# One attention kernel, two orders of the scores within a slot: two pairs and two, or three pairs and one

## The chip, the cores and the metric

The kernel runs on one core of one Trainium2 chip. The metric is the device time of one launch in microseconds (us), the median of several runs. TensorE (PE in the profile, PEld for its weight loads) multiplies matrices into PSUM. VectorE (DVE) and ScalarE (ACT) read PSUM and work element by element. GpSimd (POOL) adds a little, and SyncE (SP) issues most of the DMAs. The engines run side by side and meet only at semaphores.

## The reference

Per image of 512 tokens and 256 features (16 images, 16 heads of 16 features), with `x` in float32:

```python
q = heads(x @ Wq)
k_s, v_s = heads(x @ Wkv_short)        # keys and values of the short attention
decay_bias = -abs(pos[None, :] - pos[:, None]) * (1.0 - decay_factor)
out_short = softmax(q k_s^T / 4 + decay_bias) v_s
k_l, v_l = heads(x @ Wkv_long)
out_long = softmax(q k_l^T / 4) v_l
out = alpha * out_short + (1 - alpha) * out_long     # alpha = sigmoid(mix_weight)
x = layernorm(x + out @ Wo)
# then a gated recurrence over the 16 images, an output layer and a second layernorm
```

Both orders compute the same: first attention with the largest score of each row taken off before the exponential, then the recurrence.

## The kernel before

The launch has two phases. The attention phase (`attention_phase`) takes four fifths of the time. The recurrence phase (`recurrence_phase`) follows it and is not touched.

The attention phase handles one image per `body(b)`, with b from -1 to 16, all written out. A body has 32 **slots**. The work of an image is eight units of four heads, alternately of the long and of the short attention, each with four slots, one for each 128 keys (for the softmax) or 128 queries (for the maxima). Slots 0 to 3 are long, 4 to 7 short, and so on. A slot does this:

- **Two pairs of scores for the softmax.** `scores_of(b, s, hp)` multiplies keys by queries for heads `2*hp` and `2*hp+1` (two matmuls of 512 columns, L551) into two PSUM banks. ACT takes the exponential of these 1024 columns into `probs` (`exp_pair`, L327). Below they are E0 and E1.
- **Two pairs of scores for maxima**, of a unit two units ahead (`AHEAD` is 8 slots). `scores_for_max` multiplies queries by keys (L577), and DVE reduces them to a maximum per row (`reduce`, L493). Below M0 and M1.
- In short slots **bias matmuls** of 64 columns (`diagonals`, L533) are added to each pair, after the E and the M of it.
- **The weighted sum of the slot before** (`weigh`, L615): probabilities times values, four matmuls of four heads in four column groups of the array, into `pv_ps`. Below W. It waits for both exponentials of its slot.
- **One task** of the table `TASKS`, which all use the one bank `work`: "v" (values, seven slots of an image: 2, 3, 4, 7, 20, 24, 28), "kq" (keys and queries, in two halves of the contraction in neighbouring slots; the second half is in slots 11, 15, 19, 23, 27, 31), "ot" (transposes, slots 0 and 6), "wo" (output projection, slots 8, 12, 16) and "turn" (slots 1, 5, ..., 29: transposes of the sum and of the maxima).

All score pairs go through three PSUM buffers `pair_ps0` to `pair_ps2` in turn (`pair_of`): the pair at position 4*s+i of the program takes buffer (4*s+i) mod 3. So each pair has to wait until the pair three positions before it has been read, by ACT's exponential for an E and by DVE's reduction for an M.

No scheduler reorders anything. What an engine does next is the order in which its function writes it:

- PE in a slot: E0, M0 (and bias), the task, E1, M1 (and bias), then W of the slot before.
- ACT in a slot: the exponential of E0, then `part_or_values`, then the exponential of E1. `part_or_values` copies a task's result out of `work` where the task is a "v" (L350), an "ot" (L338) or the second half of a "kq" (L342), which is in 15 of the 32 slots; it waits for the last matmul of that task. In slots 0, 4, ..., 28 the copy of `pv_ps` (L382) follows. In slots 25 to 28 one normalisation of 256 columns (L372) stands between, and in slot 4 the rounding of the next image's input (L356) stands first.
- DVE in a slot: the reduction of M0, what the task wants of DVE, the reduction of M1.
- SP loads keys, queries and maxima for later units.

The image b = 0 has no "ot" and "wo" tasks (they belong to the image before), and the image b = 15 none for a following image, so that there are slots without a task.

## Time and profile before

| | us |
|---|---|
| median of 3 runs | 2291.74 (2289.07 to 2291.78) |
| profiled execution | 2290.99 |
| its span | 2289.2 |
| PE busy | 2101.6 (92%) |
| DVE busy | 1663.5 (73%) |
| ACT busy | 1476.8 (65%) |
| POOL busy | 174.1 (8%) |
| granted TensorE clock, mean | 0.964 of 2.4 GHz |

Busy is the time with an instruction running. An idle engine costs nothing unless another one waits for it. A busy PE is not PE at its peak. In the chain of work that ended last, PE has 86% and ACT 5%. The profile gives start and length of each instruction, and what released an engine that had been idle.

### The profile page before, as it was taken

To read this page: it belongs to the slowest core of one execution; us is meant where nothing else is said; L and a number is where in the kernel's file an instruction comes from. 1 tells how busy PE (TensorE), PEld (TensorE's weight loads), DVE (VectorE), ACT (ScalarE), POOL (GpSimd) and SP (SyncE) were. 2 spreads that over 40 slices of the span, in tenths; PEclk is the share of its full clock that TensorE was granted. 3 is DMA by queue.
4 is the path that set the end of the run, shared out by engine and by line. 5 is a ranking of instruction groups with operands and counts; after the bars stand their busy time and mean duration, and the time that the engine had idled before them with its cause. 6 is when DMAs were issued, how large, how long until landed. Compare 5 with 4: busy or idle time off the path is not lost.

```text
span 2289.2 us, 42658 instructions
## 1 busy us (share of the span) xinstructions
PE 2101.6 (92%) x16472; PEld 1126.9 (49%) x16472; DVE 1663.5 (73%) x2106; ACT 1476.8 (65%) x1758; POOL 174.1 (8%) x203
## 2 busy tenths in 40 slices
PE   2999999999999999999999999999999869999950
PEld 1444444444444444444444444444444348888840
DVE  2788888888888888888888788888888723333367
ACT  1477777777777777777777777676767643333336
POOL 0000000000000000000000000000000000000038
PEclk8799999999999999999999999999999979999975
DMA  2222222222222222222222222222222130000017
GB/s 77 47 64 55 53 63 54 62 61 57 63 54 62 54 62 55 62 54 63 55 62 54 62 55 62 64 52 63 53 53 54 36 113 28 27 27 27 18 37 220
DMA packets 127657, 134.27 MB, mean 59 GB/s; under 512 B 39778, under 2 KB 85602, under 8 KB 127474
## 3 DMA queue, kind: packets, MB, share of 16 engines
q1 hardware_dynamic: 98306, 98.74, 18.3%
q10 hardware_dynamic: 29168, 33.03, 4.7%
q8 instruction: 121, 1.98, 0.4%
q14 instruction: 62, 0.51, 0.1%
HBM read 37.77 MB, written 16.78 MB: 24 GB/s over the span
## 4 chain that ended last, share of the span: by engine, by line
PE 86%; ACT 5%; SPq 2%; POOL 2%; issue 2%; DVE 1%; DMA 0%; ACTq 0%; POOLq 0%; DVEq 0%
PE pv_ps L615 22%; PE pair_ps L551 17%; PE work L525 14%; PE pair_ps L577 11%; PE gate_ps L1050 11%; PE work L677 4%; PE pair_ps L533 3%; PE work L1043 2%; ACT probs L327 2%; SPq L199 2%; ACT pv_sb L382 2%; POOL rstd L806 1%; POOL veps L804 1%; PE work L681 1%; PE work L1034 1%
## 5 line engine op out<-in xcount | busy, mean ns | idle before, releaser
L493 DVE TENSOR_REDUCE maxes<-pair_ps 128x2 f32<-128x1024 f32 x1024 | 1247.4, 1223 | 277.4 <-PE pair_ps L533 171.6
L327 ACT ACTIVATE probs<-pair_ps,small 128x1024 f32<-128x1024 f32 x512 | 570.0, 1114 | 250.1 <-PE pair_ps L533 242.8
L327 ACT ACTIVATE probs<-pair_ps 128x1024 f32<-128x1024 f32 x512 | 523.1, 1023 | 180.1 <-PE pair_ps L551 175.8
L615 PE MATMUL pv_ps<-probs,vals 128*32 128x512 f32 x4096 | 547.5, 607 | 0.6 <-ACT probs L327 0.5
L551 PE MATMUL pair_ps<-q_op,k_op 56*128 56x512 f32 (+1 forms) x2048 | 512.4, 498 | 3.6 <-DMA q_op<-shift_rows 2.8
L577 PE MATMUL pair_ps<-k_op,q_op 55*128 55x512 f32 x2048 | 439.4, 425 | 29.3 <-DMA q_op<-kq_l 18.4
L551 PEld LDWEIGHTS pair_ps<-q_op,k_op 56*128 56x128 f32 (+1 forms) x2048 | 191.3, 184 | 554.8 <-issue 525.2
L577 PEld LDWEIGHTS pair_ps<-k_op,q_op 55*128 55x128 f32 x2048 | 196.3, 187 | 94.4 <-ACT probs L327 34.5
L533 PE MATMUL pair_ps<-eye_b,tri_b 64*128 64x64 bf16 x4096 | 152.3, 194 | 0.0
L292 POOL TENSOR_TENSOR o_sum<-o_att 128x512 f32<-128x512 f32 x32 | 40.9, 1278 | 1306.7 <-DVE o_att L460 1306.7
L533 PEld LDWEIGHTS pair_ps<-eye_b,tri_b 64*128 64x128 bf16 x4096 | 90.4, 96 | 92.3 <-issue 72.1
L615 PEld LDWEIGHTS pv_ps<-probs,vals 128*32 128x32 f32 x4096 | 80.7, 108 | 101.6 <-issue 87.2
L525 PE MATMUL work<-xt_h,w_hi 128*128 128x512 f32 x192 | 98.4, 512 | 24.7 <-POOL xt_l L299 20.9
L833 ACT ACTIVATE act_out<-gate_ps,bias 128x512 f32<-128x512 f32 x96 | 65.3, 686 | 73.6 <-PE gate_ps L1050 73.6
L677 PE MATMUL work<-ident_sb,pv_sb 128*128 128x128 f32 x512 | 80.8, 281 | 27.6 <-ACT pv_sb L382 20.9
L441 DVE SCALAR_TENSOR_TENSOR kq_l<-work,kq_h 128x512 fp32r<-128x512 f32 x96 | 66.4, 692 | 46.1 <-ACT kq_h L342 46.1
L918 DVE TENSOR_TENSOR xs_l<-work,xs_h 128x512 fp32r<-128x512 f32 x32 | 20.6, 686 | 104.0 <-ACT xs_h L842 104.0
L842 ACT ACTIVATE xs_h<-work 128x512 fp32r<-128x512 f32 x32 | 17.4, 595 | 115.3 <-PE work L1034 111.9
L382 ACT ACTIVATE pv_sb<-pv_ps 128x512 f32<-128x512 f32 x128 | 76.5, 597 | 22.8 <-PE pv_ps L615 15.7
L525 PE MATMUL work<-wv_hi,xt_h 128*128 128x256 f32 x256 | 84.4, 330 | 1.5 <-DVE kq_l L441 1.4
L677 PEld LDWEIGHTS work<-ident_sb,pv_sb 128*128 128x128 f32 x512 | 53.8, 141 | 60.0 <-issue 53.4
L342 ACT ACTIVATE kq_h<-work 128x512 fp32r<-128x512 f32 x96 | 56.9, 593 | 33.8 <-PE work L525 29.5
(129 smaller groups left out, 2467.9 us busy)
## 6 DMA issues: line engine op xcount, KB each, us to landing
k_op<-kq_h SPq DMA_DIRECT2D x1024, 32.0 KB, 2.0
k_op<-kq_l SPq DMA_DIRECT2D x512, 32.0 KB, 2.0
q_op<-kq_h SPq DMA_DIRECT2D x512, 32.0 KB, 2.0
x_step<-in_xT ACTq DMA_DIRECT2D x16, 512.0 KB, 4.1
q_op<-kq_l SPq DMA_DIRECT2D x256, 32.0 KB, 2.0
x_res<-in_x ACTq DMA_DIRECT2D x16, 512.0 KB, 4.6
x_dram<-res ACTq DMA_DIRECT2D x16, 512.0 KB, 3.4
x_back<-x_dram SPq DMA_DIRECT2D x16, 512.0 KB, 4.8
```

Of the source, the lines that this page charges most:

```text
L327: act.activation(probs[:, s % 2, 2 * hp:2 * hp + 2, :], pairs_ps[pair_of(b, s, 2 * hp)][:, :, :], ACT.Exp, scale=LAM if s // 4 % 2 else 1. ...
L382: act.activation(pv_sb[:, u % 2, :], pv_ps[:, :], ACT.Copy).then_inc(pv_copied, 1)
L441: dve.scalar_tensor_tensor(dst, work[:, :], scale, hi.bitcast(F32), ALU.mult, ALU.subtract).then_inc(done[kind], 1)
L493: dve.reduce_max(maxes[:, u % 2, :, hp, s % 4], pairs_ps[pair_of(b, s, 2 * hp + 1)][:, :, :], mybir.AxisListType.X).then_inc(a_reduced, 1)
L525: last = pe.matmul(out, lhs(a, k), rhs(c, k), start=(k == 0 and a + c == 0), stop=(k == KC - 1 and c == 1))
L533: yield pe.matmul(bank[:, P * chunk + HALF * half:P * chunk + HALF * half + HALF], tri_b[at:at + HALF, which, half, :], eye_b[at:at + HALF ...
L551: last = pe.matmul(banks[:, j, :], k[HALF * j:HALF * j + rows, hp, P * c:P * c + P], q[HALF * j:HALF * j + rows, hp, :], start=True, stop= ...
L577: last = pe.matmul(banks[:, j, :], q[at:at + MAX_ROW, hp, P * c:P * c + P], k[at:at + MAX_ROW, hp, :], start=True, stop=u % 2 == 0)
L615: last = pe.matmul(pv_ps[32 * h:32 * h + 32, :], vals[:, c, g // 2, att, at:at + 32], probs[:, s % 2, h, :], start=(c == 0), stop=(c == TC ...
L677: last = pe.transpose(work[:, P * t:P * t + P], pv_sb[:, sums[1] % 2, P * t:P * t + P], id_sb[:, :])
L833: act.activation(act_out[:, k, g, :], gate_ps[n][:, :], ACT.Tanh, bias=bias[:, g, k:k + 1], scale=0.5 if g < 2 else 1.0).then_inc(gate_don ...
L1050: last = pe.matmul(gate_ps[n][:, :], lhs[a][:, g, k, P * mc:P * mc + P], rhs[d][:, k, :], start=start and m == 0, stop=stop and m == len(p ...
```

## The change

On PE, a slot becomes E0, M0, bias of both, M1, its bias, W of the slot before, E1, its bias, and then the task. Two functions name the pair that held a buffer before (`held`) and the slot that is weighed (`weighed`). The pairs keep taking the three buffers in turn, so with the order E0, M0, M1, E1 the pair three positions back is now: for E0 the M0 of the slot before, for M0 the M1 of the slot before, for M1 the E1 of the slot before, for E1 the E0 of the same slot. DVE reduces M0 and M1 before its part of the task. ACT's order is as it was: exponential of E0, `part_or_values`, exponential of E1. `LAG` (1) and `PROBS` (2) are what had been written as numbers.

```diff
@@ def pair_of / new functions
+def held(b, s, i):
+    for back in (PAIRS, 2 * PAIRS):
+        slot, j = divmod(4 * (b * SLOTS + s) + i - back, 4)
+        bb, ss = divmod(slot, SLOTS)
+        weights = j in (0, 3)
+        if exists(bb if weights else unit_of(bb, (ss + AHEAD) // 4)[0]):
+            return weights, bb, ss, j // 2
+    return None
+def weighed(b, s):
+    return (b, s - LAG) if s >= LAG else (b - 1, s - LAG + SLOTS)
@@ ACT, exp_pair
-                wait(act, pv_full, b, SLOTS, s - 1)
-                act.activation(probs[:, s % 2, 2 * hp:2 * hp + 2, :], pairs_ps[pair_of(b, s, 2 * hp)][:, :, :], ACT.Exp,
+                wait(act, pv_full, b, SLOTS, s - PROBS + 1)
+                act.activation(probs[:, (b * SLOTS + s) % PROBS, 2 * hp:2 * hp + 2, :], pairs_ps[pair_of(b, s, 3 * hp)][:, :, :], ACT.Exp,
@@ DVE, body
-                            dve.reduce_max(maxes[:, u % 2, :, hp, s % 4], pairs_ps[pair_of(b, s, 2 * hp + 1)][:, :, :],
+                            dve.reduce_max(maxes[:, u % 2, :, hp, s % 4], pairs_ps[pair_of(b, s, 1 + hp)][:, :, :],
...
                     reduce(0)
+                    reduce(1)
                     if has_task(b, s):
...
-                    reduce(1)
@@ PE, waits of a pair
+            def banks_free(b, s, i):
+                last = held(b, s, i)
+                if last:
+                    weights, bb, ss, hp = last
+                    if weights:
+                        wait(pe, exp_done, bb, 2 * SLOTS, 2 * ss + hp + 1)
+                    else:
+                        wait(pe, a_reduced, bb, 2 * SLOTS, 2 * (ss + AHEAD) + hp + 1)
+                return pairs_ps[pair_of(b, s, i)]
@@ PE, body
             def body(b):
                 for s in range(SLOTS):
                     scores(b, s, 0)
-                    if has_task(b, s):
-                        work_task(b, s)
+                    scores_for_max(b, s, 0)
+                    bias(b, s, 0)
+                    bias_for_max(b, s, 0)
+                    scores_for_max(b, s, 1)
+                    bias_for_max(b, s, 1)
+                    weigh(*weighed(b, s))
                     scores(b, s, 1)
-                    bb, ss = (b, s - 1) if s else (b - 1, SLOTS - 1)
-                    if exists(bb):
-                        weigh(bb, ss)
+                    bias(b, s, 1)
+                    work_task(b, s)
```

PE before, in slot 3 of the first image and at the first pair of slot 4 (L551 an E, L577 an M, L525 the value task, L615 the weighted sum):

```order
L551 MATMUL pair_ps0<-q_op0,k_op0 128x512 x2
L577 MATMUL pair_ps1<-k_op2,q_op1 128x512 x2
L525 MATMUL work<-wv_hi,xt_h0 128x256
L525 MATMUL work<-wv_hi,xt_l0 128x256
L525 MATMUL work<-wv_lo,xt_h0 128x256
L525 MATMUL work<-wv_hi,xt_h0 128x256
L525 MATMUL work<-wv_hi,xt_l0 128x256
L525 MATMUL work<-wv_lo,xt_h0 128x256
L551 MATMUL pair_ps2<-q_op0,k_op0 128x512 x2
L577 MATMUL pair_ps0<-k_op2,q_op1 128x512 x2
L615 MATMUL pv_ps<-probs,vals 32x512 x4
L551 MATMUL pair_ps1<-q_op0,k_op1 128x512 x2
```

PE after, from the last pair of slot 2 (its first row, then the value task of slot 2) to the weighted sum in slot 3 (L578 an E, L601 an M, L545 the task, L635 the weighted sum):

```order
L578 MATMUL pair_ps2<-q_op0,k_op0 128x512 x2
L545 MATMUL work<-wv_hi,xt_h0 128x256
L545 MATMUL work<-wv_hi,xt_l0 128x256
L545 MATMUL work<-wv_lo,xt_h0 128x256
L545 MATMUL work<-wv_hi,xt_h0 128x256
L545 MATMUL work<-wv_hi,xt_l0 128x256
L545 MATMUL work<-wv_lo,xt_h0 128x256
L578 MATMUL pair_ps0<-q_op0,k_op0 128x512 x2
L601 MATMUL pair_ps1<-k_op2,q_op1 128x512 x2
L601 MATMUL pair_ps2<-k_op2,q_op1 128x512 x2
L635 MATMUL pv_ps<-probs,vals 32x512 x4
```

The task stood between two groups of an E and an M, and now stands at the end of the slot, after the last E. The second M of slot 3 takes `pair_ps2`, which holds the last E of slot 2, and only the task, an E and an M lie between the two. Before, the second M of slot 3 took `pair_ps0`, which held the first E of the same slot, issued ahead of the task; and between the last E of a slot and the M that took its buffer stood an M, a weighted sum and an E.

ACT before, from the exponential of slot 2's first E on (L327 an exponential, L350 the copy of the values out of `work`):

```order
L327 ACTIVATE probs<-pair_ps2 128x1024
L350 ACTIVATE vals<-work 128x2x8x16
L327 ACTIVATE probs<-pair_ps1 128x1024
L327 ACTIVATE probs<-pair_ps0 128x1024
L350 ACTIVATE vals<-work 128x2x8x16
L327 ACTIVATE probs<-pair_ps2 128x1024
```

ACT after, from the exponentials of slot 1 on (L347 an exponential, L370 the copy of the values):

```order
L347 ACTIVATE probs<-pair_ps1 128x1024 x2
L347 ACTIVATE probs<-pair_ps2 128x1024
L370 ACTIVATE vals<-work 128x2x8x16
L347 ACTIVATE probs<-pair_ps2 128x1024
L347 ACTIVATE probs<-pair_ps0 128x1024
```

Nothing has moved on ACT but the buffers that it reads: the copy of slot 2's values still stands between the exponentials of slot 2, and the one behind the copy reads `pair_ps2`.

## Rows read from the trace of the kernel before

**Rows 1.** Windows: busy us (instructions) of each engine, PE's clock, DMA.
```profile
core 0: us, PE busy (x) PEld busy (x) DVE busy (x) ACT busy (x) POOL busy (x), PEclk, DMA share, GB/s
500.00:1000.00 500.00, 491.66 (x4167) 234.11 (x4169) 411.99 (x482) 370.81 (x424) 29.82 (x30) 1.00 0.25 58
```

**Rows 2.** Waits: engine, line, released by: us in total, times, longest.
```profile
PEld pair_ps L577 <- ACT probs L327: 34.5, 78, 1.2
...
PE work L677 <- ACT pv_sb L382: 20.9, 33, 2.6
...
PE pair_ps L577 <- ACT probs L327: 8.4, 13, 0.8
```

**Rows 3.** Timeline: start us, us, instruction; long slot with "kq" task.
```profile
699.79 0.50 PE L525 MATMUL work<-xt_h,w_hi 128*128 128x512 f32 x1
...
700.68 0.50 PE L551 MATMUL pair_ps<-q_op,k_op 56*128 56x512 f32 x2
...
700.79 0.60 ACT L342 ACTIVATE kq_h<-work 128x512 fp32r<-128x512 f32 x1
...
701.02 0.40 PE L577 MATMUL pair_ps<-k_op,q_op 55*128 55x512 f32 x2
...
701.28 1.02 ACT L327 ACTIVATE probs<-pair_ps 128x1024 f32<-128x1024 f32 x1
...
701.35 1.07 PE L615 MATMUL pv_ps<-probs,vals 128*32 128x512 f32 x8
...
702.35 0.50 PE L551 MATMUL pair_ps<-q_op,k_op 57*128 57x512 f32 x2
```

**Rows 4.** Timeline: short slot without a task, first image.
```profile
101.75 0.50 PE L551 MATMUL pair_ps<-q_op,k_op 57*128 57x512 f32 x2
...
102.09 0.40 PE L577 MATMUL pair_ps<-k_op,q_op 55*128 55x512 f32 x2
...
102.32 0.29 PE L533 MATMUL pair_ps<-eye_b,tri_b 64*128 64x64 bf16 x8
...
102.45 0.48 PE L551 MATMUL pair_ps<-q_op,k_op 57*128 57x512 f32 x2
...
102.61 1.11 ACT L327 ACTIVATE probs<-pair_ps,small 128x1024 f32<-128x1024 f32 x1 [0.68 <-PE pair_ps L533]
...
103.77 0.51 PE L577 MATMUL pair_ps<-k_op,q_op 55*128 55x512 f32 x2 [0.84 <-ACT probs L327]
```

**Rows 5.** Timeline: end of a value task and its copy.
```profile
399.18 0.50 PE L551 MATMUL pair_ps<-q_op,k_op 57*128 57x512 f32 x2
...
399.34 0.38 ACT L350 ACTIVATE vals<-work 128x256 f32<-128x256 f32 x1
```

**Rows 6.** Timeline: slots 28 and 29, ACT's copy of `pv_ps` and the turn.
```profile
401.12 0.59 ACT L372 ACTIVATE res<-res,nmr,rstd 128x256 f32<-128x256 f32 x1
...
402.18 0.60 ACT L382 ACTIVATE pv_sb<-pv_ps 128x512 f32<-128x512 f32 x1 [0.47 <-ACT res L372]
...
402.93 0.63 PE L677 MATMUL work<-ident_sb,pv_sb 128*128 128x128 f32 x4 [1.02 <-ACT pv_sb L382]
```

**Rows 7.** Timeline: end of a turn and DVE's part of it.
```profile
403.59 0.50 PE L551 MATMUL pair_ps<-q_op,k_op 57*128 57x512 f32 x2
...
403.70 0.28 DVE L450 TENSOR_SCALAR shift_rows<-work 16x128 fp32r<-16x128 f32 x1 [0.52 <-PE work L681]
...
404.18 0.42 DVE L460 TENSOR_TENSOR o_att<-work,rden 128x256 f32<-128x256 f32 x1
```

**Rows 8.** Groups by line: count, then busy us, mean ns, idle before us.
```profile
L493 DVE TENSOR_REDUCE maxes<-pair_ps 128x2 f32<-128x1024 f32 x1024 | 1247.4, 1223 | 277.4 <-PE pair_ps L533 171.6 <-PE pair_ps L577 96.3
...
L356 ACT ACTIVATE xt_h<-x_step 128x1024 fp32r<-128x1024 f32 x16 | 16.8, 1049 | 0.0
```

**Rows 9.** Windows, columns as in rows 1: first maxima, and last image.
```profile
66.00:81.00 15.00, 12.12 (x64) 6.83 (x63) 12.52 (x13) 1.59 (x3) 0.00 (x0) 0.50 0.21 47
1811.00:1826.00 15.00, 12.11 (x139) 5.46 (x137) 11.10 (x16) 9.47 (x9) 1.59 (x4) 1.00 0.11 37
```

More of the change, by code:

```diff
@@ L55 @@
          8: ("wo", (0,), -1), 12: ("wo", (1,), -1), 16: ("wo", (2, 3), -1), 20: ("v", (0, 1), 1), 24: ("v", (2,), 1), 28: ("v", (3,), 1)}
-TASKS |= {10 + 4 * i + half: ("kq", (n, half), 1) for i, n in enumerate(KQ_ORDER) for half in range(2)}
+TASKS |= {10 + 4 * i + half: ("kq", (n, (half,)), 1) for i, n in enumerate(KQ_ORDER) for half in range(2)}
 TASKS |= {4 * m + 1: ("turn", m, 0) for m in range(UNITS)}
+LAG, PROBS = 1, 2
 XT_SLOT, XT_LOAD_SLOT = 4, 10
@@ L338, in part_or_values @@
                     act.activation(ot_h[:, n, :], work[:, :], ACT.Copy).then_inc(ot_hi, 1)
-                if kind == "kq" and n[1]:
+                if kind == "kq" and 1 in n[1]:
                     m = n[0]
@@ L492, in reduce @@
                             wait(dve, a_full, bb, 8 * UNITS, 8 * u + 2 * (s % 4) + hp + 1)
-                            dve.reduce_max(maxes[:, u % 2, :, hp, s % 4], pairs_ps[pair_of(b, s, 2 * hp + 1)][:, :, :],
+                            dve.reduce_max(maxes[:, u % 2, :, hp, s % 4], pairs_ps[pair_of(b, s, 1 + hp)][:, :, :],
                                            mybir.AxisListType.X).then_inc(a_reduced, 1)
                     reduce(0)
+                    reduce(1)
                     if has_task(b, s):
                         kind, n, off = TASKS[s]
-                        if kind == "kq" and n[1]:
+                        if kind == "kq" and 1 in n[1]:
                             m = n[0]
@@ L552, in scores_of @@
                                      start=True, stop=u % 2 == 0)
-                return last, banks
+                if u % 2 == 0:
+                    last.then_inc(b_full, 1)
             def scores_for_max(b, s, hp):
@@ L558, in scores_for_max @@
                 c = s % 4
+                if not exists(bb):
+                    return
                 q, k = q_op[u // 2], k_op[u % RING]
-                banks = pairs_ps[pair_of(b, s, 2 * hp + 1)]
                 if c == 0 and hp == 0:
@@ L563, in scores_for_max @@
                     wait(pe, q_loaded[u // 2], bb, 192, 192)
-                    if isinstance(bb, int) and bb == 0 and u == 0:
+                    if bb == 0 and u == 0:
                         pe.wait_ge(rows_set, 16 * 4 * RING)
@@ L568, in scores_for_max @@
                         pe.wait_ge(ones_set, 1)
-                if exists(b):
-                    wait(pe, exp_done, b, 2 * SLOTS, 2 * s + hp)
-                else:
-                    wait(pe, a_reduced, b, 2 * SLOTS, 2 * (s + AHEAD) - 2 + hp)
+                banks = banks_free(b, s, 1 + hp)
                 for j in range(2):
@@ L578, in scores_for_max @@
                                      start=True, stop=u % 2 == 0)
-                return last, banks
+                if u % 2 == 0:
+                    last.then_inc(a_full, 1)
             def diagonals(banks, which, c):
@@ L585, in diagonals, with bias, bias_for_max @@
                 return last
-            def scores(b, s, hp):
-                c, short = s % 4, s // 4 % 2
-                here, later = exists(b), exists(unit_of(b, (s + AHEAD) // 4)[0])
-                if here:
-                    b_last, b_banks = scores_of(b, s, hp)
-                    if not short:
-                        b_last.then_inc(b_full, 1)
-                if later:
-                    a_last, a_banks = scores_for_max(b, s, hp)
-                    if not short:
-                        a_last.then_inc(a_full, 1)
-                if short and here:
-                    diagonals(b_banks, 1, c).then_inc(b_full, 1)
-                if short and later:
-                    diagonals(a_banks, 0, c).then_inc(a_full, 1)
+            def bias(b, s, hp):
+                if s // 4 % 2 and exists(b):
+                    diagonals(pairs_ps[pair_of(b, s, 3 * hp)], 1, s % 4).then_inc(b_full, 1)
+            def bias_for_max(b, s, hp):
+                if s // 4 % 2 and exists(unit_of(b, (s + AHEAD) // 4)[0]):
+                    diagonals(pairs_ps[pair_of(b, s, 1 + hp)], 0, s % 4).then_inc(a_full, 1)
             def weigh(b, s):
+                if not exists(b):
+                    return
                 u, c = s // 4, s % 4
@@ L614, in weigh @@
                     at = VW * (GH * (g % 2) + h)
-                    last = pe.matmul(pv_ps[32 * h:32 * h + 32, :], vals[:, c, g // 2, att, at:at + 32], probs[:, s % 2, h, :],
+                    last = pe.matmul(pv_ps[32 * h:32 * h + 32, :], vals[:, c, g // 2, att, at:at + 32], probs[:, (b * SLOTS + s) % PROBS, h, :],
                                      start=(c == 0), stop=(c == TC - 1))
@@ L639, in work_task @@
             def work_task(b, s):
+                if not has_task(b, s):
+                    return
                 kind, n, off = TASKS[s]
@@ L649, in work_task @@
                 if kind == "kq":
-                    m, half = n
+                    m, ks = n
                     w, cols = (1, 0, 2)[m % 3], m // 3
                     last = three(work[:, :], lambda a, k: (w_hi, w_lo)[a][:, w, k, P * cols:P * cols + P],
-                                 lambda a, k: xt[a][:, k, :], (half,))
-                    if half:
+                                 lambda a, k: xt[a][:, k, :], ks)
+                    if 1 in ks:
                         last.then_inc(full["kq"], 1)
```

15 lines of the change are left out of this document (6 added, 9 removed).

## The prediction

> **What bounds the kernel now.** I read the windows first. In 500 us of steady state PE is busy for 491.7 us, DVE for 412.0 and ACT for 370.8, at full granted clock [rows 1]. So PE sets the pace of the attention phase, and what reorders PE can gain no more than PE's waits, while everything that makes PE wait is paid in full. Then the waits of PE: 20.9 us for the copy of `pv_ps`, 8.4 us of matmuls and 34.5 us of weight loads for exponentials [rows 2], 64 us in 16 images, and some of the weight loads' part is hidden behind the matmul before. The third view is the timeline, for what a wait on ACT is made of. The gain is thus small, and the question is whether a new wait comes.
>
> **The new chain.** Three facts meet. ACT is in order: in slots 28 and 29 the copy of `pv_ps` starts only at 402.18, behind a normalisation of another tensor that began at 401.12, and PE's turn waits 1.02 us for it [rows 6]. ACT's order in a slot is exponential of E0, copy of the task's result, exponential of E1. And the change puts E1 ahead of the task, and gives E1's buffer to the second M (M1) of the next slot. So where a task's result is copied by ACT, in 15 of 32 slots, the exponential of an E1 that has long been ready stands behind a copy that waits for the end of the task, and PE, done with the task, comes to the next M1 after only an E and an M. Before the change the weighted sum of 1.00 us (701.35 to 702.35) [rows 3] stood between the two as well and covered this.
>
> Let the task end at 0 (the next E starts there).
>
> - ACT: the copy starts at 0.11 (700.68 to 700.79) or 0.16 (399.18 to 399.34) [rows 3, 5]; I take 0.15. The exponential behind a "kq" or "ot" copy starts 0.49 after it (700.79 to 701.28) [rows 3]; behind a value copy of 0.38 in place of 0.60 [rows 3, 5] it is 0.22 less, 0.27. It lasts 1.02 in a long slot and 1.11 in a short one [rows 3, 4]. A waiting M starts 0.05 after its end (102.61 + 1.11 = 103.72, 103.77) [rows 4]. Sum for "kq" and "ot": 1.71 long, 1.80 short. For values: 1.49 and 1.58.
> - PE: an E takes 0.34 to the next M [rows 3]. An M takes 0.33 before W (701.02 to 701.35) and 0.23 before bias matmuls (102.09 to 102.32) [rows 3, 4]. M to M isn't in these rows; those are its bounds. So PE is at the long M1 at 0.57 to 0.67, I take 0.62. In a short slot 8 bias matmuls come in between; the next E came 0.13 behind them (102.32 to 102.45) [rows 4], and with up to 0.1 more it is 0.70 to 0.80, I take 0.75.
>
> The stall is the difference, with the exponential's length of the task's slot and PE's way of the next one. "ot": slot 0 1.09, slot 6 1.05. "kq": 0.96 in each of 11, 19, 27 (long, next short), 1.18 in each of 15, 23, 31. That is 8.6 us an image. Values: 2 and 24 0.87 each, 3 0.74, 4 and 28 0.83 each, 7 0.96, 20 with two copies 0.83 + 0.27 = 1.10. That is 6.2 us. Together **14.8 us an image**. In the 17 other slots the exponential of E1 starts as soon as E1 is done: 0.60 us after E1's start (700.68 to 701.28) and 1.02 long, it ends at 1.62 [rows 3]. PE comes to the next M1 after E1, the task's 0.89 (699.79 to 700.68) [rows 3] and 0.62, at 1.85. No wait, though with only 0.2 us to spare.
>
> **What comes with it.**
>
> - A weight load behind a late wait is exposed by some 0.1 us in front of bias matmuls (M to bias 0.23 against 0.33 to its end): 8 short M1, +0.8.
> - W of the first slot of a unit waits for ACT's copy of `pv_ps`, which stands behind the late exponential: about 0.49 (as after a "kq" copy) less the 0.33 of M1, 0.16 in slots 0 and 24; in 28 a normalisation stands in between, +0.48. In slot 4 the 1.05 us of the next input's rounding [rows 8] come behind a late exponential and ahead of that of E0, and E1 waits for it by about 0.45. Sum about +1.2, with 0.4 for small ones 1.6.
> - DVE: after a turn it is busy until 404.18 + 0.42 = 404.60, 1.01 after the turn's end [rows 7], and then has two reductions of 1.23 [rows 8], since both now follow one another: 3.47. PE wants the buffer of the second, for M0 two slots on, a slot and an E later; a long slot takes 0.89 + 2 x 0.67 + 1.00 = 3.23 [rows 3], so at 3.57. It just fits. Where DVE's part is longer (the output task of two chunks in slot 16) I estimate a wait of 0.6, and with what is handed on to the neighbours 1.1 an image. DVE's order alone costs nothing in the 15 slots, since they become longer.
>
> Sum of what is added: 14.8 + 0.8 + 1.6 + 1.1 = **18.3 us an image**.
>
> **What goes.** Of the 64 us of waits the turn's for the copy goes (the turn stands at the slot's end now), and part of the M's for exponentials: I take half of 64 us, 2.1 an image (all: 4.0, none: 0). **What only moves.** The matmuls are the same. Per slot the old order has twice E, M; the new one E, M, M and a single E. An M that follows an M may take 0.23 or 0.33; a bias group is split in two, which may cost up to 0.1 a slot. Bounds: -3.2 to +1.6 an image; I take -0.8, nearer to the row of M before bias matmuls. SP's loads: keys and queries wait for the E of a unit, which is not later than before relative to its slot, and the maxima's rows are loaded from a turn half a slot later, with two longer slots ahead of their use. I cost both at nothing; the cover is those two slots, over 6 us.
>
> Net: 18.3 - 2.1 - 0.8 = **+15.4 us an image**. Fourteen images pay it in full, 216 us. The first has 13 of the 15 copies (13 us), the last 6 (5 us). The tail and the recurrence don't change. The profiled execution took 2290.99 us, in the span of the median's runs (2289.07 to 2291.78), so 2291 + 234 = **2525 us**.
>
> **PE's clock.** In the new stretches PE idles some 1.05 of 4.3 us. In the last image it was busy for 12.11 of 15 us, with waits of 0.8 us as in rows 4, and the granted clock stayed at 1.00, 2.4 GHz; with the first maxima it was busy just as long and the clock was 0.50, 1.2 GHz, from the start on [rows 9]. So a clock that has risen holds at such a share, and I cost this at nothing.
>
> The Trainium skill ("TensorE: Matmul & The Clock Gate", Part 1) says that the default state is throttled and that activity releases the throttle, which speaks against a change that makes PE idle more often. By that rule the clock could fall in the stalled stretches; the trace agrees that there are two levels, and shows none of it at gaps of this size.
>
> **The rivals.**
>
> 1. **No wait, and PE's own waits go.** If the exponential of E1 ended before PE comes to the next M1, the change would only take the old waits and shorten the order: -4.0 and -0.8 an image at best, 2291 - 16 x 4.8 = 2214; with my values 2291 - 16 x 2.9 = 2245 us. It decides at the copy plus exponential, 1.5 to 1.8 us against 0.6 to 0.8 on PE. The stall would have to be under 2.9 / 15 = 0.19 us instead of 1.0. For it: nothing in ACT's rows. Against: the order of ACT and rows 6. Chance 3%.
> 2. **A smaller price.** The order itself saves its full 3.2 us, all old waits go, and DVE's and the small ones don't come: 14.8 + 0.8 - 3.2 - 4.0 = 8.4 an image, 2291 + 15.2 x 8.4 = 2419 us. Chance 6%.
> 3. **The delays add up on ACT.** ACT's late exponential of E1 also delays that of the next E0, for which E1 waits. By the rows it ends at 0.15 + 0.49 + 0.91 + 1.02 = 2.6 (0.91 being an exponential less 0.11 of overlap, as 0.49 is 0.60 less 0.11), and E1 starts at 1.71 + 0.33 + 1.00 = 3.0. If this margin of 0.4 is lost, or the 0.2 of the other slots, each of the 15 slots pays 0.5 more: 2525 + 15 x 0.5 x 15.2 = 2640 us. Chance 7%.
> 4. **The clock falls** to 1.2 GHz in the stalled slots. Then PE's 3.2 us of work in each would take twice as long, less about half a stall that hides in it: +2.6 us for 15 slots and 15.2 images, 2525 + 590 = 3115 us; in parts of them less. Chance 4%.
>
> That the change doesn't do what it says is excluded by the rows of the order.
>
> **How the numbers follow.** My forecast has 80% and its own range is 2450 to 2600: with -3.2 for the order and nothing for the small terms and DVE it is 14.8 + 0.8 - 3.2 - 2.1 = 10.3 an image, 2448; with +1.6, DVE's part doubled and no more than 1.3 gained 18.3 + 1.1 + 1.6 - 1.3 = 19.7, 2590. The other four lie outside on both sides and hold 20%, so the range stays. A measurement of this kernel can tell about 0.2%, 4.6 us. Slower by more: the forecast and rivals 2 to 4, 96% with a little left out for a mistake of kind, 0.95; faster 0.04; same 0.01.
>
> **What the profile after would show.** PE's waits for the exponentials before M (new L601), matmuls and weight loads together, at some 200 to 260 us and 240 times or so, about 1.0 us each, and only after tasks that ACT copies; slots after "turn", "wo" and first halves of "kq" as long as before, 3.2 and 3.5 us, those after copies 4.1 to 4.6; PE's busy time about as before, its share of the span down to 83 to 85%; ACT's time before an exponential no longer released by the E of the same slot there, but ACT busy without a break from the copy on; clock at 1.00. Wrong would be: M1 waiting for DVE instead, waits in all slots, or a granted clock under 0.95 in the middle.

## The result and the profile after

| | before | after |
|---|---|---|
| median | 2291.76 us (4 runs, 2289.07 to 2292.08) | 2567.47 us (4 runs, 2557.60 to 2574.41) |
| ratio | | 1.1203, 95% interval 1.1164 to 1.1242 |
| span of the profiled execution | 2289.2 us | 2567.6 us |
| granted TensorE clock, mean | 0.964 | 0.954 |

The change makes the kernel 276 us slower. I had forecast 2525 us, and 2450 to 2600.

The page of the kernel after: busy time and share of each engine, PE's granted clock in 40 slices, the shares of the chain that ended last, and two groups of instructions (count, busy us, mean ns, idle time before them and what ended it).

```profile
PE 2180.0 (85%) x16472; PEld 1143.9 (45%) x16472; DVE 1641.7 (64%) x2106; ACT 1440.6 (56%) x1758; POOL 173.8 (7%) x203
...
PEclk8799999999999999999999999999999996999985
...
PE 72%; ACT 13%; issue 6%; DVE 5%; POOL 2%; SPq 1%; ACTq 1%; DMA 0%; POOLq 0%; DVEq 0%
...
L601 PE MATMUL pair_ps<-k_op,q_op 55*128 55x512 f32 x2048 | 428.4, 442 | 227.5 <-ACT probs L347 192.2
...
L370 ACT ACTIVATE vals<-work 128x256 f32<-128x256 f32 x128 | 47.8, 386 | 243.7 <-PE work L545 243.7
```

PE's busy share fell from 92% to 85%. In the chain that ended last PE has 72%, where it had 86%, and ACT 13%, where it had 5%. ACT was idle for 243.7 us ahead of the value copies (L370), waiting for PE's task. In the kernel before it was 36.2 us (us in total, times, longest):

```profile
ACT vals L350 <- PE work L525: 36.2, 33, 20.1
```

That is the mark of the new chain: an in-order engine standing at an instruction whose input is late, while what others need is behind it.

The waits of PE (us in total, times, longest), which answer to [rows 2]:

```profile
PE pair_ps L601 <- ACT probs L347: 192.2, 233, 1.0
...
PE pv_ps L635 <- ACT pv_sb L402: 19.1, 16, 2.5
PE pair_ps L601 <- DVE maxes L513: 15.7, 31, 2.0
```

The second M of a slot (L601) waits 192.2 us in 233 instances for exponentials; the same M waited 8.4 us in 13 before [rows 2]. The weight loads before them sat idle through the same stretches and don't count twice.

One instance in the timeline (start us, us, instruction): slot 2 of an image, whose task is a value task, and what follows.

```profile
1249.03 0.28 PE L545 MATMUL work<-wv_lo,xt_h 128*128 128x256 f32 x1
...
1249.23 0.50 PE L578 MATMUL pair_ps<-q_op,k_op 56*128 56x512 f32 x2
1249.34 0.39 ACT L370 ACTIVATE vals<-work 128x256 f32<-128x256 f32 x1 [1.79 <-PE work L545]
...
1249.57 0.40 PE L601 MATMUL pair_ps<-k_op,q_op 55*128 55x512 f32 x2
1249.62 1.94 ACT L347 ACTIVATE probs<-pair_ps 128x1024 f32<-128x1024 f32 x2
...
1250.69 0.49 PE L601 MATMUL pair_ps<-k_op,q_op 55*128 55x512 f32 x2 [0.72 <-ACT probs L347]
...
1251.12 1.06 PE L635 MATMUL pv_ps<-probs,vals 128*32 128x512 f32 x8
```

The last matmul of the task starts at 1249.03, and the next E at 1249.23. ACT's copy of the values starts 0.11 behind that, the first of two exponentials (x2, the one of slot 2's last E and the one of the next first E) at 1249.62, 0.28 behind the copy, as forecast from [rows 3, 5]. It ends after 1.02, at 1250.64, and M starts 0.05 later. PE had been ready for it 0.24 after the other M, at 1249.81. (Where nothing waits, as in slot 2 of the same image, the two M in a row take 0.58 us to the weighted sum, 0.24 and 0.34: an M before an M costs what an M before bias matmuls costs in [rows 4].)

To see where the time sits I took the spans between the starts of successive weighted sums in the timeline, "W(s) to W(s+1)". In the new order each holds the last E and the task of slot s+1 and the first three pairs of slot s+2. In the kernel before, W ends the slot, so the same span is the whole of slot s+2 with that slot's task. The column "before" thus has another task in it than the row names; it compares the place in the image, and e1_exp_first (below) has the same task. The medians over the 14 inner images:

| span, and task in it (new order) | before | after | e1_exp_first |
|---|---|---|---|
| W(8) to W(9), turn | 3.21 | 3.07 | 3.07 |
| W(9) to W(10), first half of "kq" | 3.21 | 3.22 | 3.22 |
| W(10) to W(11), second half of "kq" | 3.57 | 4.50 | 3.52 |
| W(2) to W(3), value | 3.59 | 4.29 | 3.53 |
| W(5) to W(6), "ot" | 3.58 | 4.35 | 3.29 |
| W(3) to W(4), value, rounding of the input | 3.59 | 4.98 | 3.96 |
| W(27) to W(28), value, normalisation, copy of `pv_ps` | 4.34 | 5.61 | 4.78 |
| whole image, where the clock stays up | 110.9 | 126.8 | 112.4 |

Spans whose task ACT doesn't copy are as long as before or up to 0.2 us shorter, but for one: W(16) to W(17), behind the double output task of slot 16, is 3.72 us where it was 3.23, since an M waits 0.44 for DVE. (That double task itself stands in W(15) to W(16), 3.93 us, and stood in W(14) to W(15) before, 4.02.) Those with a copy in the table are longer than before by 0.7 to 1.4 us, and longer than in e1_exp_first by 0.8 to 1.1.

### The profile page after: what moved, and what is told of

It is laid out like the page before. It is cut to its first block, busy times and chain, and to the rows that moved or that the text cites. A ratio compares the mean times of both kernels' runs of the same rounds, so it can differ in the third digit from the quotient of the medians.

```text
span 2567.6 us, 42643 instructions
## 1 busy us (share of the span) xinstructions
PE 2180.0 (85%) x16472; PEld 1143.9 (45%) x16472; DVE 1641.7 (64%) x2106; ACT 1440.6 (56%) x1758; POOL 173.8 (7%) x203
## 4 chain that ended last, share of the span: by engine, by line
PE 72%; ACT 13%; issue 6%; DVE 5%; POOL 2%; SPq 1%; ACTq 1%; DMA 0%; POOLq 0%; DVEq 0%
PE pv_ps L635 19%; PE pair_ps L578 12%; PE work L545 12%; ACT probs L347 11%; PE gate_ps L1075 10%; PE pair_ps L601 10%; DVE maxes L513 3%; PE work L699 3%; PE pair_ps L553 2%; PE work L1068 2%; SPq L219 1%; PE work L686 1%; ACT xt_h L376 1%; POOL rstd L831 1%; POOL veps L829 1%
## 5 line engine op out<-in xcount | busy, mean ns | idle before, releaser
L513 DVE TENSOR_REDUCE maxes<-pair_ps 128x2 f32<-128x1024 f32 x1024 | 1213.3, 1219 | 336.8 <-PE pair_ps L553 209.5
L347 ACT ACTIVATE probs<-pair_ps,small 128x1024 f32<-128x1024 f32 x512 | 568.9, 1115 | 187.4 <-PE pair_ps L553 186.6
L601 PE MATMUL pair_ps<-k_op,q_op 55*128 55x512 f32 x2048 | 428.4, 442 | 227.5 <-ACT probs L347 192.2
L347 ACT ACTIVATE probs<-pair_ps 128x1024 f32<-128x1024 f32 x512 | 522.3, 1024 | 165.2 <-PE pair_ps L578 160.2
L635 PE MATMUL pv_ps<-probs,vals 128*32 128x512 f32 x4096 | 559.4, 618 | 25.3 <-ACT pv_sb L402 19.1
L578 PE MATMUL pair_ps<-q_op,k_op 56*128 56x512 f32 (+1 forms) x2048 | 518.1, 505 | 7.1 <-ACT probs L347 7.0
L578 PEld LDWEIGHTS pair_ps<-q_op,k_op 56*128 56x128 f32 (+1 forms) x2048 | 193.8, 186 | 572.8 <-ACT probs L347 422.6
L601 PEld LDWEIGHTS pair_ps<-k_op,q_op 55*128 55x128 f32 x2048 | 196.9, 190 | 314.5 <-ACT probs L347 261.2
L553 PE MATMUL pair_ps<-eye_b,tri_b 64*128 64x64 bf16 x4096 | 200.1, 197 | 0.0
L370 ACT ACTIVATE vals<-work 128x256 f32<-128x256 f32 x128 | 47.8, 386 | 243.7 <-PE work L545 243.7
L553 PEld LDWEIGHTS pair_ps<-eye_b,tri_b 64*128 64x128 bf16 x4096 | 107.5, 97 | 154.9 <-issue 139.6
L635 PEld LDWEIGHTS pv_ps<-probs,vals 128*32 128x32 f32 x4096 | 83.6, 108 | 116.4 <-issue 89.0
L545 PE MATMUL work<-xt_h,w_hi 128*128 128x512 f32 x192 | 97.5, 508 | 24.6 <-POOL xt_l L319 20.9
L470 DVE TENSOR_SCALAR shift_rows<-work 16x128 fp32r<-16x128 f32 x128 | 35.4, 277 | 117.3 <-PE work L703 117.3
L699 PE MATMUL work<-ident_sb,pv_sb 128*128 128x128 f32 x512 | 89.9, 302 | 1.4 <-DVE ot_l L461 1.4
L943 DVE TENSOR_TENSOR xs_l<-work,xs_h 128x512 fp32r<-128x512 f32 x32 | 20.6, 686 | 104.1 <-ACT xs_h L867 104.1
L545 PE MATMUL work<-wv_hi,xt_h 128*128 128x256 f32 x256 | 84.5, 330 | 1.4 <-DVE kq_l L461 1.4
```

What stands on the lines that cost most here:

```text
L347: act.activation(probs[:, (b * SLOTS + s) % PROBS, 2 * hp:2 * hp + 2, :], pairs_ps[pair_of(b, s, 3 * hp)][:, :, :], ACT.Exp, scale=LAM if ...
L513: dve.reduce_max(maxes[:, u % 2, :, hp, s % 4], pairs_ps[pair_of(b, s, 1 + hp)][:, :, :], mybir.AxisListType.X).then_inc(a_reduced, 1)
L545: last = pe.matmul(out, lhs(a, k), rhs(c, k), start=(k == 0 and a + c == 0), stop=(k == KC - 1 and c == 1))
L553: yield pe.matmul(bank[:, P * chunk + HALF * half:P * chunk + HALF * half + HALF], tri_b[at:at + HALF, which, half, :], eye_b[at:at + HALF ...
L578: last = pe.matmul(banks[:, j, :], k[HALF * j:HALF * j + rows, hp, P * c:P * c + P], q[HALF * j:HALF * j + rows, hp, :], start=True, stop= ...
L601: last = pe.matmul(banks[:, j, :], q[at:at + MAX_ROW, hp, P * c:P * c + P], k[at:at + MAX_ROW, hp, :], start=True, stop=u % 2 == 0)
```

## The clock after slot 28

An image takes 126.8 us in four of the 14 inner images, and 128.3 to 129.9 us in the other ten. The difference is TensorE's clock. The timeline from slot 28 to 30 of one of the ten:

```profile
708.65 0.49 PE L601 MATMUL pair_ps<-k_op,q_op 55*128 55x512 f32 x2 [0.68 <-ACT probs L347]
...
709.56 0.60 ACT L402 ACTIVATE pv_sb<-pv_ps 128x512 f32<-128x512 f32 x1 [0.48 <-ACT res L392]
...
710.30 1.13 PE L635 MATMUL pv_ps<-probs,vals 128*32 128x512 f32 x8 [1.09 <-ACT pv_sb L402]
...
711.36 0.80 PE L578 MATMUL pair_ps<-q_op,k_op 57*128 57x512 f32 x2
```

Two waits follow one another within 2.3 us, 0.68 for the exponential and 1.09 for ACT's copy of `pv_ps`, and behind them an E runs for 0.80 instead of 0.50 us. The windows around it, with the granted clock as the third value from the end (PE's busy us stands first):

```profile
704.70:710.30 5.60, 3.84 (x42) 2.02 (x39) 3.77 (x4) 3.53 (x6) 0.00 (x0) 1.00 0.22 49
710.30:714.70 4.40, 4.39 (x31) 2.15 (x31) 1.05 (x4) 1.98 (x2) 0.00 (x0) 0.60 0.53 158
714.70:719.30 4.60, 4.60 (x33) 1.79 (x31) 2.36 (x2) 2.10 (x2) 0.00 (x0) 0.64 0.01 2
719.30:730.00 10.70, 8.70 (x69) 3.37 (x67) 7.70 (x8) 6.68 (x9) 0.00 (x0) 1.00 0.16 36
```

And the same stretch of an image in which the clock held:

```profile
1222.50:1228.00 5.50, 3.84 (x42) 1.99 (x38) 3.67 (x4) 3.44 (x6) 0.00 (x0) 1.00 0.25 58
1228.00:1234.00 6.00, 5.90 (x56) 2.75 (x58) 3.42 (x6) 4.10 (x4) 0.00 (x0) 1.00 0.41 112
```

In the stretch with the two waits PE was busy for 3.84 us of 5.60 and of 5.50, the same, and the clock was still 1.00 (2.4 GHz). Behind it it fell to 1.2 GHz for some 3 to 7 us in ten images and in four it didn't. Those ten cost 27 us together (their lengths less 126.8). In one of them the clock was down at the start of the image too. There it was not two waits in a row but the single waits of the M in slots 0 and 1, 4.1 us apart:

```profile
208.04 0.49 PE L601 MATMUL pair_ps<-k_op,q_op 55*128 55x512 f32 x2 [1.03 <-ACT probs L347]
...
212.14 0.51 PE L601 MATMUL pair_ps<-k_op,q_op 55*128 55x512 f32 x2 [0.94 <-ACT probs L347]
```

```profile
212.80:216.20 3.40, 3.40 (x15) 1.16 (x11) 1.37 (x2) 1.60 (x2) 0.00 (x0) 0.50 0.09 19
```

The same two waits stand at this place in the other inner images, where the clock held.

## The experiments

**e1_exp_first: ACT's order alone.**

```diff
@@ ACT, body, on the changed kernel
                     if exists(b):
                         exp_pair(b, s, 0)
+                        exp_pair(b, s, 1)
                     part_or_values(b, s)
-                    if exists(b):
-                        exp_pair(b, s, 1)
```

> The changed kernel with one edit on ACT: both exponentials of a slot first, then the copy of the task's result. Theory (ACT's order: the exponential of E1 stands behind a copy that waits for the task): the waits of the second M for exponentials, about 1 us in 15 slots of an image, go, and with them the falls of the clock in slots 28 and 29. An image, 126.8 us without such falls, loses 14.8 + 0.8, and is 109 to 113 us; some may come back since DVE's part of a key task starts 0.5 later and M0 two slots on waits for the second reduction. Time 2245 to 2320 us, granted clock back at 0.96. Rival (the new succession of the buffers, or DVE's two reductions in a row, is what costs): the waits stay or move to DVE, over 2450 us.

Measured: 2319.17 us (2317.43 to 2322.57), ratio to before 1.0131 (1.0114 to 1.0148). With PE's and DVE's new order untouched, 248 of the 276 us are gone. An image is 112.4 us in all 14 inner images, and the clock didn't fall in any. So it was ACT's order against PE's, as the theory says, and not the succession of the buffers. PE's waits now (L600 is the M and L577 the E in this kernel):

```profile
PE pair_ps L600 <- DVE maxes L512: 27.1, 67, 2.0
...
PE pv_ps L634 <- ACT pv_sb L401: 18.4, 16, 2.5
...
PE pair_ps L577 <- ACT probs L347: 4.8, 18, 0.4
```

An exponential holds an M back no more. What is left above the kernel before is 1.5 us an image, and the waits that stand there are for DVE and for the copy of `pv_ps`: the time is at the upper end of what was expected, for the reason given there. The timeline of slots 31 and 0 shows it: DVE's part of the key task starts only at 1206.39, its two reductions at 1207.00, and the second ends at 1209.35; the first M of slot 1 was due 0.34 after the E of 1208.44 and starts at 1209.40.

```profile
1206.39 0.69 DVE L460 SCALAR_TENSOR_TENSOR kq_l<-work,kq_h 128x512 fp32r<-128x512 f32 x1 [1.17 <-ACT kq_h L362]
...
1207.00 2.35 DVE L512 TENSOR_REDUCE maxes<-pair_ps 128x2 f32<-128x1024 f32 x2
...
1208.44 0.51 PE L577 MATMUL pair_ps<-q_op,k_op 56*128 56x512 f32 x2
...
1209.40 0.73 PE L600 MATMUL pair_ps<-k_op,q_op 55*128 55x512 f32 x4 [0.46 <-DVE maxes L512]
```

**e6_copy_then_part: the copy of `pv_ps` ahead of the task's copy.**

```diff
@@ ACT, body, on e1_exp_first
+                    (copy of pv_ps, where s % 4 == 0)
                     part_or_values(b, s)
                     (normalisation, slots 25 to 28)
-                    (copy of pv_ps, where s % 4 == 0)
```

> As e1_exp_first, and in the first slot of a unit the copy of pv_ps stands right behind the exponentials, ahead of the task's copy and of the normalisation. Theory: the weighted sum of slots 0, 4, ..., 28 no longer waits for that copy; 0 to 3 us an image less than e1_exp_first, 0 to 45 us in all. Rival: no difference, since that copy had time to spare once the exponentials are early.

Measured: 2323.29 us (2320.06 to 2325.12), an image 112.6 us. No gain, rather 0.2 us an image more. The span W(27) to W(28) fell from 4.78 to 3.67 us and the next rose from 3.39 to 4.47: the wait for the copy went, and the next E waited for an exponential behind the normalisation instead. The rival was right on the time, not on the reason; the wait moved.

**e2_before_exp_first: the same swap in the kernel before, as a control.**

```diff
@@ ACT, body, on the kernel before: the same lines as in e1_exp_first
```

> Control: the kernel before with ACT's exponentials first and the task's copy behind them. There the E1 is issued behind the task, so the exponential of E1 never waited for the copy, and the copy now comes about 1 us later. Theory: DVE's part of a key or transpose task waits for that copy and the reduction of the second M stands behind it; E1 of the next slot waits about 0.9 us in 8 slots of an image: slower, 2330 to 2420 us. Rival (exponentials first are simply the better order on ACT): 2291 us or less.

Measured: 2390.15 us (2388.08 to 2392.21), ratio 1.0436 (1.0415 to 1.0457), an image 117.4 us. Exponentials first are not a better order by themselves. Each of ACT's orders fits one of PE's. The time is in the range; the place only in part: DVE's late part of a task holds up PE's next task (35.6 us in 76 instances), more than its late reductions hold up an E (24.8 in 90). As much again is the turn's wait for the copy of `pv_ps`, 35.6 us in 65 instances where it was 20.9 [rows 2]. The theory left it out.

**e3_task_before_last: how much work lies between E1 and the M that takes its buffer.**

```diff
@@ PE, body, on the changed kernel
                     weigh(*weighed(b, s))
+                    work_task(b, s)
                     scores(b, s, 1)
                     bias(b, s, 1)
-                    work_task(b, s)
```

> The changed kernel with the task ahead of the last E of the slot instead of behind it. Theory (what counts is how much PE work lies between an E1 and the M that takes its buffer): the exponential of E1 ends 1.6 us after the start of E1, PE comes to the next M1 after two E and an M, at 0.95 to 1.1: a wait of 0.6 to 0.75 in all 32 slots, 20 to 23 us an image instead of 15.6. Slower than the changed kernel, 2620 to 2700 us. Rival (only the task's copies cost, whatever lies between): the copies no longer hold the exponential for long, 15 slots x 0.3 us less, about 2490 us.

Measured: 2632.93 us (2631.65 to 2634.21), an image mostly 132 to 133 us, in the range of the theory and 140 us off the rival's. The wait is shorter and in nearly every slot, 499 instances of 0.59 us on average:

```profile
PE pair_ps L601 <- ACT probs L347: 295.4, 499, 0.7
```

The clock has a part in the time that the theory didn't count. Around W(28), at waits of 0.53 us for the exponential and 1.07 to 1.11 for the copy of `pv_ps`, it fell in 13 of the 14 inner images. The one image without a fall is 131.3 us, 4.5 more than 126.8, and the falls add some 20 us to the whole, without which the time would be a little under the range.

The copy isn't needed for a wait. The chain is the exponential of E1, 1.6 us from E1's start, against the work that PE has in hand before it wants the buffer.

**e5_dve_old: DVE's order as before.**

```diff
@@ DVE, body, on the changed kernel
                     reduce(0)
-                    reduce(1)
                     if has_task(b, s):
...
                             add_rows(b + off, *n)
+                    reduce(1)
```

> The changed kernel with DVE's order as before: reduction of M0, DVE's part of the task, reduction of M1. The task now ends the slot, and M0 of the next slot takes the buffer of M1. Theory: M0 waits until DVE has done its part of the task and then the reduction, about 2.0 us after a turn (8 slots), 2.2 after a key or transpose task (8 slots, of which 1.0 is waited for already), 2 after the output tasks (3): some 30 us an image more, 2950 to 3100 us. If DVE had time to spare: no difference.

Measured once: 3589.4 us, an image 194.6 us. The direction and the place are right, M waits for reductions; the amount is far beyond what was expected.

```profile
PE pair_ps L601 <- DVE maxes L513: 557.6, 301, 2.6
```

```profile
1000.00:1500.00 500.00, 391.84 (x2367) 164.07 (x2367) 234.73 (x272) 208.72 (x244) 16.60 (x16) 0.77 0.14 34
1500.00:2000.00 500.00, 393.05 (x2364) 166.43 (x2362) 233.64 (x275) 203.69 (x237) 15.82 (x19) 0.76 0.14 33
```

With these waits of up to 2.6 us the granted clock was 0.76 to 0.77 on the mean of 500 us, so nearly half of the time at 1.2 GHz (the windows' columns are as above). I had counted the waits and not the clock. How the excess divides between the two wasn't separated.

**e4_copy_before_norm: one of the two waits ahead of the fall of the clock.**

```diff
@@ ACT, body, on the changed kernel
+                    (copy of pv_ps, where s % 4 == 0)
                     (normalisation, slots 25 to 28)
-                    (copy of pv_ps, where s % 4 == 0)
```

> The changed kernel with one edit: in slot 28 ACT copies pv_ps ahead of the normalisation and its DMA. The weighted sum of slot 29 waits 1.08 us for that copy now, right after a wait of 0.68 us, and in 10 of the 14 inner images the clock is at 1.2 GHz for the 3 to 7 us behind this. If the two waits together are what lets the clock fall: 16 us for the wait and 27 for the clock, about 2524 us, and clock 1.00 in slots 28 to 30 of all images. If the clock falls for another reason there: 2551 us.

Measured: 2548.26 us (2543.01 to 2551.95), between the two expectations, and both were wrong in half. The waits:

```profile
PE pair_ps L601 <- ACT probs L347: 192.2, 233, 1.0
PE pair_ps L578 <- ACT probs L347: 21.6, 34, 1.0
```

The wait for the copy is gone from the span W(27) to W(28), which fell from 5.61 to 4.54 us. It came back in the next, 4.43 us where 3.39 is free of waits, as a wait of the E for its exponential: 21.6 us against 7.0 after the change. An image without a fall is 126.8 us, unchanged. But the two waits now lie a weighted sum apart, and in the profiled execution the clock fell there in one of the 14 inner images, not in ten; in one more it fell behind the single waits in slots 0 and 1 (1.02 and 0.94 us). All that was gained is the clock, some 20 us.

**e10_norm29: the normalisation taken out of slot 28.**

```diff
@@ constants and ACT, body, on the changed kernel
-NORM_SLOT = 25
+NORM_SLOTS = (25, 26, 27, 29)
...
-                    if 0 <= s - NORM_SLOT < TC and exists(b - 1):
-                        t = s - NORM_SLOT
+                    if s in NORM_SLOTS and exists(b - 1):
+                        t = NORM_SLOTS.index(s)
```

> The changed kernel with the last normalisation of an image and its DMA in slot 29 instead of slot 28. In e4_copy_before_norm the wait of 1.07 us for the copy came back as a wait of the next E for its exponential, since normalisation and DMA issue stayed in front of that. Slot 29 has no copies, and ACT has about 1.2 us there. If their time on ACT in slot 28 is the cause, both waits go: 1.07 us an image less than 126.8, and no fall of the clock, 2567 - 17 - 27, about 2524 us. If the wait moves again, to slot 30: 2540 to 2550 us.

Measured: 2533.85 us (2532.38 to 2534.00). The clock falls in no inner image: 126.3 us each, and the window shows it at 1.00 with the same waits in the other slots (the next two of 500 us, up to 2000, show 1.00 as well):

```profile
500.00:1000.00 500.00, 444.58 (x3665) 207.15 (x3659) 355.77 (x421) 313.13 (x369) 26.05 (x28) 1.00 0.22 52
```

Of the 1.07 us of wait 0.5 came back in slot 30 (W(29) to W(30) is 4.12 instead of 3.59). So 34 us less: 27 for the clock and 0.5 in 15 images. Together with e4_copy_before_norm this shows that the pair of waits in slots 28 and 29 is what let the clock fall there: ten of 14 images with the pair, one with a weighted sum between the waits, none with the second wait gone. The waits of 0.6 to 1.0 us in the other slots, no more than one in a slot, seldom did: twice in the 42 inner images of these two kernels and the changed one, both times behind the waits in slots 0 and 1. What decides in which images it falls stays open.

**e8_before_copy_first and e9_before_norm29: the same two edits in the kernel before.** The diffs are those of e4_copy_before_norm and e10_norm29.

> The kernel before with one edit: in slot 28 ACT copies pv_ps ahead of the normalisation and its DMA instead of behind them. The turn of slot 29 waits 1.02 us for that copy, 0.8 us of it felt. If ACT's order is what holds PE there, 12 to 15 us less, 2277 to 2280 us; if something else was late next, no change.

Measured: 2290.53 us (2289.80 to 2292.01), ratio 1.0002 (0.9993 to 1.0011): no change; an image is 111.1 us where it was 110.9. The turn's wait fell from 20.9 to 5.7 us, and M's wait for exponentials rose from 8.4 to 20.6 [rows 2]:

```profile
PE pair_ps L577 <- ACT probs L327: 20.6, 27, 0.9
...
PE work L677 <- ACT pv_sb L374: 5.7, 19, 1.5
```

> The kernel before with the same edit. Slots 28 and 29 take 4.34 us together with the turn's wait of 1.02 us, where others with a turn take 3.57. e8_before_copy_first only moved that wait. If it goes now: 0.77 us in 15 images, 2291 - 12, about 2279 us. If it moves again: 2291 us.

Measured: 2283.16 us (2281.55 to 2283.93), ratio 0.9967 (0.9955 to 0.9979). An image is 110.5 us instead of 110.9: W(27) to W(28) 3.58 instead of 4.34, W(28) to W(29) 3.91 instead of 3.58. Less than expected, since again a part came back, but faster than both kernels:

```profile
PE pair_ps L577 <- ACT probs L327: 10.5, 26, 0.8
...
PE work L677 <- ACT pv_sb L382: 5.7, 19, 1.5
```

**e11_exp_first_norm29_xt6: the best of the new order.**

```diff
@@ constants, on e1_exp_first, with the edit of e10_norm29
-XT_SLOT, XT_LOAD_SLOT = 4, 10
+XT_SLOT, XT_LOAD_SLOT = 6, 10
```

> e1_exp_first with the last normalisation in slot 29 and the rounding of the next image's input in slot 6 instead of 4, where ACT is not behind a late copy. In e1_exp_first an image takes 112.4 us; the slots concerned take 4.78 and 3.96 us there where 3.4 and 3.5 would be free of waits. Expected 112.4 - 1.3 - 0.4 = 110.7 us an image, 2319 - 26, about 2293 us: level with the kernel before. What is left then are waits for DVE after key tasks. If the waits only move: 2310 to 2320 us.

Measured: 2314.31 us (2313.38 to 2315.14), a miss: 111.9 us an image, not 110.7. W(27) to W(28) lost 1.05 us and W(29) to W(30) took 0.52; W(3) to W(4) lost 0.32 and W(5) to W(6) took 0.35. I had counted what goes and not what is late next.

**e12_short_rest: is it DVE that holds e1_exp_first?** DVE's part of the key tasks is cut to 64 of 512 columns, so the low parts of keys and queries are left out for the others.

```diff
@@ DVE, setup and rest(), on e1_exp_first
+            dve.memset(kq_l[:, :, :, :].bitcast(F32), 0.0)
...
-                dve.scalar_tensor_tensor(dst, work[:, :], scale, hi.bitcast(F32), ALU.mult, ALU.subtract).then_inc(done[kind], 1)
+                n_ = 64 if kind == "kq" else L
+                dve.scalar_tensor_tensor(dst[:, 0:n_], work[:, 0:n_], scale, hi.bitcast(F32)[:, 0:n_], ALU.mult, ALU.subtract).then_inc(done[kind], 1)
```

> e1_exp_first, with DVE's part of a key task cut to 64 of its 512 columns (the low part of keys and queries is left out for the others, so less is computed). It asks what holds e1_exp_first above the kernel before: there M0 of slot 25 waits 0.3 us for a reduction that DVE began late, behind its part of the key task of slot 23, and the spans behind slots 23 and 31 are 3.64 us where 3.22 would be free of waits. If DVE is the cause: those spans about 3.25, an image 111.2 to 111.7 instead of 112.4 us, 2300 to 2308 us. If ACT's order or the buffers are: no change, 2319 us.

Measured: 2317.94 us (2317.16 to 2320.48), an image 112.2 us. Only W(23) to W(24) changed, 3.64 to 3.47.

```profile
1176.96 0.22 DVE L462 SCALAR_TENSOR_TENSOR kq_l<-work,kq_h 128x64 fp32r<-128x64 f32 x1 [1.17 <-ACT kq_h L362]
...
1177.10 2.35 DVE L514 TENSOR_REDUCE maxes<-pair_ps 128x2 f32<-128x1024 f32 x2
...
1179.35 0.50 PE L579 MATMUL pair_ps<-q_op,k_op 56*128 56x512 f32 x2
...
1179.69 0.62 PE L602 MATMUL pair_ps<-k_op,q_op 55*128 55x512 f32 x4
...
1179.73 0.60 ACT L401 ACTIVATE pv_sb<-pv_ps 128x512 f32<-128x512 f32 x1
...
1180.48 1.07 PE L636 MATMUL pv_ps<-probs,vals 128*32 128x512 f32 x8 [0.17 <-ACT pv_sb L401]
```

DVE's reductions start 0.5 earlier in the slot, and the M of 1179.69 follows its E after 0.34 without a wait. But the weighted sum waits 0.17 for the copy of `pv_ps`, which ACT does at 1179.73, behind the values. Behind slot 31 the span stayed as it was (3.63), and the timeline shows the same: the wait moved. The first two M of slot 1 start at 1207.85, 0.49 after their E instead of 0.96, and then the weighted sum waits 0.42 for the copy of `pv_ps`, which ends at 1208.90 (its row names no releaser; the first weighted sum of a unit has to wait for this copy):

```profile
1207.85 0.72 PE L602 MATMUL pair_ps<-k_op,q_op 55*128 55x512 f32 x4
...
1208.29 0.61 ACT L401 ACTIVATE pv_sb<-pv_ps 128x512 f32<-128x512 f32 x1
...
1208.99 1.07 PE L636 MATMUL pv_ps<-probs,vals 128*32 128x512 f32 x8 [0.42 <-issue]
```

So DVE is one of two things that are late there, and taking it away alone brings 0.2 of the 1.5 us.

## Why the prediction was right, and where it was short

- **What bounds the kernel: right.** The change could gain only PE's waits, and what came on top was paid in full.
- **The new chain: right, in place and size.** The copy starts 0.11 us after the task's end, its exponential 0.28 later, M 0.05 after that. Forecast 14.8 us an image for 15 slots and 0.8 for weight loads; undoing ACT's side takes away 14.4, net of the waits for DVE that come up in its place. Single spans in front of a short slot, after less e1_exp_first: second half of "kq" 0.98 (stall of 0.96 forecast), a value task from long to short 0.76 (0.74), "ot" in a short slot 1.06 (1.05). In front of a long slot it is more than the forecast's stall: second half of "kq" 1.30 (1.18), the value task of slot 2 0.98 (0.87). There the late weight load shows: a late M takes 0.43 to the weighted sum (1250.69 to 1251.12) where one on time takes 0.33, and this was not in the sum. In front of bias matmuls, where 0.1 for each of 8 had been added, a late second M takes 0.34 and one on time 0.32. So the 0.8 us stood at the wrong slots, and that the total fits is luck. The counts: 233 waits, about 240 forecast.
- **What comes with it: the copy of slot 28 was too low.** I had put 0.48 for it; PE waits 1.09 there. The DMA issue of 0.40 us stands on ACT between the normalisation and the copy, and I had left it out, though in [rows 6] the copy starts 1.06 after the normalisation. DVE's term was 1.1 an image; the total of 15.7 us looks like it, but only 6.1 of it are in the 14 inner images, all of it behind slot 16, where the span grew by 0.49 (a wait of 0.6 forecast). The rest is in the first maxima, the first image and the last. In slot 4 the E waits 0.38 us, 0.45 forecast.
- **What goes and what moves: right in the net only.** Of the 64 us of waits the turn's 20.9 for the copy of `pv_ps` were to go. They moved: the weighted sum waits 19.1 us for the same copy. In their place the turn's spans became shorter, by 0.14 to 0.20 us each (3.07 where it was 3.21), seven in an image, more than the 0.8 put down for the order; the first halves of "kq" take 3.22 as before. Net an image: +15.9 where the clock holds, +15.4 forecast. The single terms of this part weren't measured apart.
- **The clock: wrong.** I had costed it at nothing, since it held in the last image at the same busy share as with the first maxima [rows 9], and had taken the waits as evenly spread. Those two rows don't show the same load: 12.12 us busy at 0.50 are 64 instructions, 12.11 us at 1.00 are 139. The step that failed is the look at one slot at a time: slots 28 and 29 have two waits in a row, and there it fell. That was rival 4, in a small part of its size: 27 us, not 590.
- **The first and the last image** cost 15.2 and 9.6 us more, forecast 13 and 5.

Sum of the misses in the profiled executions, 2290.99 and 2569.41 us, which lie 278.4 apart where 234 were forecast: 14 x 0.5 = 7 us for an image's length, 27 for the clock, 7 for the outer images, 1.5 for a later start of the first weighted sum, and 2.5 behind the last one, 45 for the 44 missing.

Rival 1 (faster) is excluded: even e1_exp_first, which is its condition, is slower than the kernel before. The 2245 us that I gave it were too low, since they left out that DVE's part and the copy of `pv_ps` become late when the task ends the slot. Rival 3 (delays that add up on ACT) showed in slot 4 only, where it had been counted.

## What to carry to other kernels

When work is reordered on one engine, lay the unchanged orders of the others beside it: what an in-order engine waits for must be issued before what stands behind it is needed. Here PE's E, M, task, E, M with ACT's exponential, copy, exponential fit, and either one changed alone costs 4 to 12%. A stall that a block of work causes on a busy in-order engine came back at the next instruction behind it when the block was only swapped with its neighbour (e4, e6, e8). It went when the block moved to where that engine has room, and even then only in part: 0.3 of 0.8 us came back in e9_before_norm29 and 0.5 of 1.07 in e10_norm29.

## What the runs showed of the hardware

- The clock fell from 2.4 to 1.2 GHz behind two waits of 0.7 and 1.1 us with one M and its bias between them (3.84 us busy of 5.6), in ten of 14 images. With single waits of up to 1.0 us, one in a slot and in up to three slots running, it mostly stayed up, but fell once in this kernel and once in e4_copy_before_norm behind waits of 1.02 to 1.03 and 0.94 us in neighbouring slots. In the first window of 15 us of [rows 9] it was at 1.2 GHz throughout though PE was busy for 12.1 us. With the waits of e5_dve_old, up to 2.6 us, it was down for nearly half of the time. So a short stall can cost more than itself: 27 us for the clock beside some 16 for the wait (1.07 in 15 images).
- The Trainium skill ("TensorE: Matmul & The Clock Gate", Part 1) says that activity releases a throttle that is the default. These runs agree with that, with 1.2 GHz at the first maxima and behind the waits of slots 28 and 29, and the forecast, which gave a fall 4%, had weighed it too low.
- From start to start at 2.4 GHz an M takes 0.24 us to a following M and 0.33 to the weighted sum, an E takes 0.34 to a following M, though both are pairs of matmuls on the same rows of the array. An M that had to wait takes 0.43 to the weighted sum. Why an E differs from an M isn't shown here.
